# Feed-forward matmuls in pairs of 64-row halves, with one score pair at a time between them

## What is computed

```python
xn = _layernorm(x)
q, k, v = split(xn @ Wq + bq), split(xn @ Wk + bk), split(xn @ Wv + bv)
scores = jnp.einsum('bhnd,bhmd->bhnm', _rope(q), _rope(k)) / jnp.sqrt(256)
inter = jnp.einsum('bhnm,bhmd->bhnd', softmax(scores), v)
attn = merge(inter) @ Wo + bo
h = s0 * (concat([xn, -xn]) @ pm1(k0))      # pm1: True is 1, False is -1
h = s1 * (relu(h) * 2 @ pm1(k1))
h = s2 * (relu(h) * 2 @ pm1(k2))
out = x + attn + h                          # feed-forward 256 -> 1024 -> 1024 -> 256
```

## Time and profile before

| | us |
|---|---|
| median of 3 runs | 2984.65 (2983.89 to 2989.23) |
| the profiled execution | 2983.02 |
| its span, first to last instruction | 2981.2 |
| PE busy | 2785.1, 93% |
| ACT busy | 2146.0, 72% |
| DVE busy | 1057.8, 35% |
| mean granted TensorE clock | 0.973 of full |

### The profile page before, as it was taken

The page is one execution under the profiler, slowest core; times in us unless marked ns, Lnnn a source line. Parts: engine busy times, 40 slices in busy tenths (PEclk is TensorE's granted clock), DMA queues, the critical chain, the costliest instruction groups (busy, mean ns, idle before and its releaser), DMA issues.

```text
span 2981.2 us, 48065 instructions
## 1 busy us (share of the span) xinstructions
PE 2785.1 (93%) x16839; PEld 1300.0 (44%) x16839; DVE 1057.8 (35%) x1609; ACT 2146.0 (72%) x2301; POOL 376.9 (13%) x309
## 2 busy tenths in 40 slices
PE   6777299999999999999999999999999999999997
PEld 3443144444444444444444444444444444444444
DVE  7999422323232323232232323232322223232322
ACT  4446277777777777777777777777777777777773
POOL 5888300000000000000000000000000000000000
PEclk9999699999999999999999999999999999999998
DMA  6666411112121212112122212121211212221212
GB/s 200 196 196 191 131 43 44 43 47 55 47 50 41 61 45 73 49 46 62 48 65 54 69 44 69 39 75 45 63 53 51 62 47 66 54 69 43 74 35 96
DMA packets 279684, 211.62 MB, mean 71 GB/s; under 512 B 183616, under 2 KB 227392, under 8 KB 272960
## 3 DMA queue, kind: packets, MB, share of 16 engines
q1 hardware_dynamic: 271040, 200.30, 24.6%
q10 hardware_dynamic: 8448, 8.39, 0.9%
HBM read 132.08 MB, written 76.55 MB: 70 GB/s over the span
## 4 chain that ended last, share of the span: by engine, by line
PE 79%; issue 6%; DMA 2%; SPq 1%; DVE 1%; POOL 0%; ACT 0%; POOLq 0%; DVEq 0%
PE ps_o L871 29%; PE ps_f L903 27%; PE ps_s L856 22%; SPq L749 1%; DMA y<-rest_sum_d 1%; POOL heads L962 0%; PE ps_f L943 0%; DMA q_rows<-row_shift 0%; DVE sums L983 0%; DMA rest_sum_d<-rest_sum 0%; DMA probs<-rest_sum_d 0%; DMA heads_t<-heads 0%; DVE k_rows L1029 0%; PE ps_o L943 0%; DVE h_hi L993 0%
## 5 line engine op out<-in xcount | busy, mean ns | idle before, releaser
L831 ACT ACTIVATE probs<-ps_s 128x1024 f32<-128x1024 f32 x2048 | 1985.8, 1022 | 620.5 <-PE ps_s L856 620.5
L871 PE MATMUL ps_o<-probs,v_ones 128*32 128x512 f32 x8192 | 992.0, 602 | 0.0
L856 PE MATMUL ps_s<-q_rows,k_rows 50*128 50x512 f32 x4096 | 797.0, 462 | 61.9 <-DMA q_rows<-row_shift 32.6
L856 PEld LDWEIGHTS ps_s<-q_rows,k_rows 50*128 50x128 f32 x4096 | 337.2, 185 | 717.3 <-ACT probs L831 468.1
L993 DVE TENSOR_SCALAR h_hi<-ps_f 128x512 fp32r<-128x512 f32 x256 | 175.7, 686 | 1102.1 <-PE ps_f L903 1101.7
L903 PE MATMUL ps_f<-h_hi,ffn_w 128*128 128x512 f32 x1024 | 425.8, 416 | 0.0
L903 PE MATMUL ps_f<-h_lo,ffn_w 128*128 128x512 f32 x1024 | 415.6, 406 | 0.0
L871 PEld LDWEIGHTS ps_o<-probs,v_ones 128*32 128x32 f32 x8192 | 214.6, 109 | 453.0 <-issue 449.6
L962 POOL TENSOR_TENSOR heads<-heads,sums 128x512 f32<-128x512 f32 x64 | 85.9, 1342 | 2240.1 <-DVE sums L983 2240.1
L903 PEld LDWEIGHTS ps_f<-h_hi,ffn_w 128*128 128x128 f32 x1024 | 192.1, 188 | 101.7 <-issue 70.1
L983 DVE RECIPROCAL sums<-sums 128x128 f32<-128x128 f32 x256 | 225.0, 920 | 1.8
(11 more groups left out here) (87 smaller groups left out, 1382.5 us busy)
## 6 DMA issues: line engine op xcount, KB each, us to landing
k_rows<-k_parts SPq DMA_DIRECT2D x128, 256.0 KB
q_rows<-q_parts SPq DMA_DIRECT2D x384, 64.0 KB
q_parts<-parts SPq DMA_DIRECT2D x32, 512.0 KB, 3.7
k_parts<-parts SPq DMA_DIRECT2D x32, 512.0 KB, 4.5
k_rows<-k_parts SPq DMA_DIRECT2D x128, 128.0 KB
x_chunk<-in_x ACTq DMA_DIRECT2D x16, 512.0 KB, 4.1
xn_t<-xnT SPq DMA_DIRECT2D x16, 512.0 KB, 4.4
v_heads<-v_sb SPq DMA_DIRECT2D x16, 512.0 KB, 5.3
```

Source lines behind the costliest of these rows:

```text
L831: nc.scalar.activation(probs[:, s % PBUF, half * 2 * C:(half + 1) * 2 * C], ps_s[:, half].rearrange("p c n -> p (c n)"), ACT.Exp, scale=SC ...
L856: last = nc.tensor.matmul(ps_s[:, half, w], k_rows[rows, u, t * P:(t + 1) * P], q_rows[rows, u, half], start=True, stop=True)
L871: last = nc.tensor.matmul(ps_o[32 * c:32 * c + 2 * DH], v_ones[:, u, t], probs[:, s % PBUF, c * C:(c + 1) * C], start=(t == 0), stop=(t == ...
```

## The change

The feed-forward matmuls of 128 rows become **pairs** of matmuls of 64 rows. In a pair, the first matmul uses rows 0 to 63 and adds into one bank, and the second uses rows 64 to 127 and adds into another bank, which belongs to the next group. After half of its pairs the two groups swap the row halves (`phase`), so that each bank gets both halves of its sum. PE waits at the swap until the matmuls of the first phase are complete (`half_done`). A pair of groups takes as many pairs as it took matmuls before (8, 32 and 32 in the three layers). The projection keeps 128 rows.

A cycle now gives its four score pairs one by one, and between them stand three **visits** of feed-forward pairs. Their sizes are in `VISITS`: 2, 2, 4 in each of the four cycles of the first layer; two projection cycles with 0, 4, 0 matmuls, which stay empty in passes without projection; then 6 pairs in a cycle of the second layer and 8 in every fifth; and 12, 10 and 10 of the half-width pairs in a cycle of the third. DVE takes both groups of a pair after the second is done. In the new file `scores` is at line 859, `beside` at 887 and `one_pass` at 934.

```diff
-def turns(with_projection):
...
+FIRST, PROJECT, SECOND, THIRD = range(4)
...
+VISITS = {FIRST: [2, 2, 4], PROJECT: [0, 4, 0], SECOND: [2] * 13 + [3] * 2, THIRD: [4] * 4 + [3] * 4 + [4]}
...
-            def scores(i, s):
+            def scores(i, s, half):
...
-                for half in range(2):
-                    pe.wait_ge(probs_ready, 2 * STEPS * i + (2 * s + half + 1))
-                    for w in range(2):
...
+                pe.wait_ge(probs_ready, 2 * STEPS * i + (2 * s + half + 1))
+                for w in range(2):
...
+                banks = (first % BANKS, (first + 1) % BANKS)
                 if m == 0:
 
-                    pe.wait_ge(group_used, before + (k_th + 2 if k_th < BANKS - 1 else k_th + 1))
-                    if n == 0:
+                    pe.wait_ge(group_used, before + (first + 3 if first == 0 else first + 2))
...
+                if m == size:
+                    pe.wait_ge(half_done, 2 * swap)
+                for w in range(2):
+                    side = (w + phase) % 2
+                    rows = slice(GROUP_ROWS * w, GROUP_ROWS * (w + 1))
+                    n = 2 * pair + side
+                    if layer == FIRST:
+                        to, lhs, rhs = ps_f[:, banks[side]], w0[rows, k, n * P:(n + 1) * P], (xT_hi, xT_lo)[low][rows, k]
...
+                    last = nc.tensor.matmul(to, lhs, rhs, start=(m == 0), stop=(m == 2 * size - 1))
+                    if m == size - 1:
+                        last.then_inc(half_done, 1)
+                    if m == 2 * size - 1:
+                        last.then_inc(group_done, 1)
...
+                for c in range(STEPS // 2):
+                    s = FFN_FROM + 2 * c
+                    more = s < STEPS or not last
+                    if more:
+                        scores(i, s, 0)
+                    for layer, pair, m in TURNS[projects][3 * c]:
+                        beside(i, projects, layer, pair, m)
+                    if more:
+                        scores(i, s, 1)
+                    for layer, pair, m in TURNS[projects][3 * c + 1]:
+                        beside(i, projects, layer, pair, m)
+                    if more:
+                        scores(i, s + 1, 0)
+                    for layer, pair, m in TURNS[projects][3 * c + 2]:
+                        beside(i, projects, layer, pair, m)
+                    if more:
+                        scores(i, s + 1, 1)
                     weigh(i, s - 2)
                     weigh(i, s - 1)
...
-                dve.wait_ge(group_done, groups_before(i, projects) + (k_th + 1))
+                dve.wait_ge(group_done, groups_before(i, projects) + (k_th + 1 if n >= GROUPS else k_th + 2 - k_th % 2))
```

More of the change, by code:

```diff
@@ L61, with pairs, number, cycles @@
 GROUPS = SUMS + TT
-def turns(with_projection):
[L66 to L87, removed]
+SWAPS = FT + TT // 2
+FIRST, PROJECT, SECOND, THIRD = range(4)
+def pairs(layer):
+    return {FIRST: FT // 2, PROJECT: TT // 2, SECOND: FT // 2, THIRD: TT // 2}[layer]
+def number(layer, pair, side):
+    return {FIRST: 0, PROJECT: GROUPS, SECOND: FT, THIRD: SUMS}[layer] + 2 * pair + side
+VISITS = {FIRST: [2, 2, 4], PROJECT: [0, 4, 0], SECOND: [2] * 13 + [3] * 2, THIRD: [4] * 4 + [3] * 4 + [4]}
+def cycles(with_projection):
+    visits, ends, order = [], [], []
+    for layer in (FIRST, PROJECT, SECOND, THIRD):
+        for pair in range(pairs(layer)):
+            at = 0
+            for count in VISITS[layer]:
+                present = layer != PROJECT or with_projection
+                visits.append([(layer, pair, at + m) for m in range(count)] if present else [])
+                at += count
+            ends += [[] for _ in VISITS[layer][::3]]
+            if layer != PROJECT or with_projection:
+                ends[-1] = [number(layer, pair, side) for side in range(2)]
+                order += ends[-1]
+    assert len(ends) == STEPS // 2
+    return visits, ends, {n: k for k, n in enumerate(order)}
+TURNS, ENDS, ORDER = zip(*(cycles(p) for p in (False, True)))
 def groups_before(i, projects):
@@ L903, in beside @@
[L903 to L916 removed]
+                if pair == 0 and layer in (SECOND, THIRD) and m in (0, 2 * (FT - 2)):
+                    sums_of = (FIRST, SECOND)[layer == THIRD]
+                    needed = FT // 2 - 1 if m else FT // 2 - 2
+                    pe.wait_ge(group_used, before + (ORDER[projects][number(sums_of, needed, 1)] + 1 + BANKS))
@@ new lines, in beside @@
+                if layer == PROJECT:
+                    side, k = m // DT, m % DT
+                    t = 2 * pair + side
+                    last = nc.tensor.matmul(ps_f[:, banks[side], 0:D], headsT[:, k, t * P:(t + 1) * P], wo[:, k],
+                                            start=(k == 0), stop=(k == DT - 1))
+                    if k == DT - 1:
+                        last.then_inc(group_done, 1)
+                    return
+                size = 2 * (DT if layer == FIRST else FT)
@@ L917, in one_pass @@
                     weigh(i, s - 2)
                     weigh(i, s - 1)
+            w0, w1, w2 = w["w0"], w["w1"], w["w2"]
             pe.sem_inc(pv_done, PBUF)
-            scores(0, 0)
-            scores(0, 1)
+            for s in range(FFN_FROM):
+                scores(0, s, 0)
+                scores(0, s, 1)
             pe.wait_ge(consts_loaded, 48)
```

58 lines of the change are left out of this document (21 added, 37 removed).

## The result

| | before | after |
|---|---|---|
| median, 5 runs each on one chip | 2984.65 (2983.89 to 2989.23) | 3001.54 (2999.9 to 3006.57) |
| the profiled execution | 2983.02 | 3001.54 |
| its span | 2981.2 | 2999.7 |
| mean granted TensorE clock | 0.973 | 0.966 |

The ratio is 1.0054, 95% interval 1.0039 to 1.0069: slower by about 16 us, small but clear of the 0.2% (6 us) that the prediction took for what a measurement can tell. The forecast was 2986, no change, with a range of its own of 2976 to 2998 and one of 2972 to 3030 with two rivals in it.

What follows compares the result with a forecast made beforehand. A chain from PE to ACT and back was taken to bound cycles at 4.90. Passes with projection -5.5, without +3.8, no-loop returns +2, empty cycles +3: +3.3 on 2983.02 gives 2986; own range 2976 to 2998, with two rivals 2972 to 3030.

Steps and rivals of the forecast that it cites:

- B: Rival: the two halves' loads don't lie side by side in a stream; third-layer pairs take 0.21, 3017 us; chance 0.12.
- C: Rival: the longer loop body makes PE wait a second time for instructions at returns with projection, 3028 us; chance 0.05.
- the first layer: Four pairs before the fourth score pair make these cycles 5.14, 0.24 above the chain; 0.96 us a pass.
- the empty cycles: Two cycles without feed-forward work in passes without projection: the clock may fall; 0 to 12 us in all, taken as 3.
- PE's excess: In passes with projection, PE's own work costs 1.42 us a pass above the chain, which the change removes.
- Second-layer cycles of 4.90: The PE-ACT chain keeps these cycles at 4.90; the 0.4 us PE saves turns into waiting for ACT.
- pairs 0.23 apart: A feed-forward pair of 512 columns costs 0.23 us, as one full matmul does; bounds 0.21 and 0.46.
- The two cycles where no loop returns: Into pass 4 and the last pass, PE waits for the first groups to be emptied: 1 us each, 2 in all.
- A: Rival: PE's total is the true bound, so saved switches shorten all 512 cycles by 0.4, 2778 us; chance 0.11.
- D: Rival: a feed-forward pair costs clearly more than a full matmul: 0.34 gives 3150 us, 0.46 gives 3470; chance 0.10.
- Two float32 matmuls take 0.59 together ... so about 0.22 each.: Projection cycles: four matmuls at about 0.22 and two switches end near 1.73, so the cycle stays at 4.90.
- Cycles 6 to 30: Second- and third-layer cycles of a pass: 11.2 us less in all with projection, no change without.

Runs made afterwards that it cites:

- e1: The changed kernel without 6 of the 32 pairs of each second-layer pair of groups (384 in all): 2998.71, ratio 1.0042 to the kernel before.
- e5: The kernel before, without 3 of 16 matmuls in every second-layer group (384 in all): 2975.75, ratio 0.9968.
- e4: The changed kernel with a cycle's two weighings apart, each behind one step's scores: 2999.75, ratio 1.0045 to the kernel before.
- e10: The changed kernel with projection moved later, empty cycles filled, and uneven second-layer cycles (8 pairs, weighings together; 4 pairs, apart): 2863.61, ratio 0.9598 to the kernel before.
- e6: The changed kernel with the empty cycles of passes without projection given to the last two pairs of first-layer groups: 2991.81, ratio 1.0031 to the kernel before.
- e7: The changed kernel with the two weighings apart only from cycle 6 of a pass on: 3006.16, ratio 1.0086 to the kernel before.
- e8: e7 with e6's filling, and second-layer groups ending in other cycles than a head does: 2986.21, ratio 1.0014 to the kernel before.

## Why the forecast was right, and where it was off

**What the number owes to luck.** The forecast was no change within 0.2%, and the change is a slowdown of 0.5%. Inside the forecast the prediction gave 0.13 to slower. The median of 3001.54 lies 3.5 us above the forecast's own range (2976 to 2998); it is inside 2972 to 3030 only because that range was made to hold rivals B and C, and neither of them came. The low end of the own range was mis-added as well: with nothing for the first layer and the empty cycles, and all of PE's excess gone, the sum gives 2983 - 17 + 2 = 2968, below the low end of the wider range too.

**The frame held.** Second-layer cycles of 4.90 with ACT as the last releaser, first-layer ones of 5.14, pairs 0.23 apart: each was forecast and is in the rows. The two cycles where no loop returns are 0.93 longer (6.07 for 5.14), forecast 1.0. Cycles with 8 pairs take 4.93 for 4.90. e1 and e5 show by taking work away that the chain bounds, e4 and e10 by breaking it, and the last pass of either kernel by a chain 0.08 shorter.

**The rivals.** A (2778) is out by the result itself, in which the switches are gone and the cycles stay at 4.90, and by e1. B is out by the third layer's timeline, where the pairs stand 0.12 apart:

```profile
1647.94 0.28 PE L928 MATMUL ps_f<-ffn_w,h_hi 64*128 64x256 f32 x2
...
1648.06 0.28 PE L928 MATMUL ps_f<-ffn_w,h_lo 64*128 64x256 f32 x2
...
1648.18 0.28 PE L928 MATMUL ps_f<-ffn_w,h_hi 64*128 64x256 f32 x2
```

C didn't come: the loop's return with projection has one gap, as before. The rows name "issue" for such a gap; that PE waits for instructions in it isn't shown. D's price of 0.34 for a pair appears only behind a wait (from the score pair at 1551.19 to the next at 1551.53); in a stream it is 0.23. The Trainium skill's page "TensorE: Matmul & The Clock Gate" (Part 3, The mechanism), which the prediction weighed, says that weight loads overlap running matmuls only where the row group differs. That doesn't fit these rows: in the pair after the pair the row groups are the same, and the loads stay hidden.

**The steps that failed** are sizes, and together they are the 15.8 us between the forecast's +3.3 and the 19.1 of the table:

- *"Two float32 matmuls take 0.59 together ... so about 0.22 each."* The two records of the earlier trace rows were one matmul. A float32 matmul of 256 columns leaves two records, and eight records (four matmuls) start 0.22 apart, so a matmul costs 0.43 and the switches the rest of the 1.92. (`turns` in the kernel before counts it as two full ones, which was there to be seen.) A projection cycle takes 5.11, not 4.90. That is 0.21 x 24 = 5.0 us. The other 1.4 of the 6.4 missed in this row of the table is mostly the wait for the load of `y`, which both kernels have in some passes: about 12 us before (what cycle 4 takes beyond its usual 5.19), 13 after (what it takes beyond 5.11). The Trainium skill ("FP8 and Floating Point Precision", TensorE Precision Notes) says that true float32 takes four passes through the array. Four times 256 columns at 2.4 GHz would be 0.43, an estimate from that page, and the trace agrees with 0.43.
- *"I take 3, nearer to nothing, because the weighing in such a cycle is as dense as before."* The empty cycles cost 6.2 in this execution: 0, 3.1, 1.5 and 1.6 in the four passes. The dense weighing didn't keep the clock up in three of them. It lay inside the bounds of 0 and 12. e6 shows that the clock is the cause; what tips it, with nearly the same waits in the first pass, stays open.
- *Cycles 6 to 30* gained 0.6 us less than forecast with projection, and without it lost 1.0: 0.03 in each cycle with 8 pairs, 64 of them, is 1.9, more than both.
- *The start of `attend`* had no term. It cost 2.5 in this execution: there the clock is at half when the first pairs come (0.43 from pair to pair), and it rose some 5 us later than before. That is mostly chance. In the profiles of e1, e6, e7 and e8, whose queue is the same there, the place lies from 0.5 under to 2.0 over before, and in that of e5, which has the queue of the kernel before, it is 2.0 over.

*The first layer* came out at +12.2 with projection for +11.1. The forecast's +3.8 without it came out at +5.1, of which 2.3 is in the first cycle after a loop's return; that cycle differs from pass to pass in both kernels (8.0 to 9.3 before, 9.1 to 10.1 after), and why was not tried.

## What to carry to other kernels

Before valuing a saving on the busiest engine, take one period of the steady state and ask what released the instruction that ends last. Here PE was busy for 93% before, after, and in a version 4% faster. Where two bounds lie within 2% of each other (a chain through another engine, and the engine's own work), relief of one alone buys next to nothing (0.3% in e5); work can then be placed unevenly, so that long blocks lie under the chain and short ones where the chain is cut. And each gain brings forward the next late thing: make a ledger by place of cycle, since e7 and e8 won what they were built for and lost it again in other cycles, for the most part on one late load.

## What the runs showed that I had not expected

- A float32 matmul stands in the trace as two records with the shape of the whole (eight for the projection's four, sixteen for the eight of two weighings). Count records against the program before dividing a duration by them.
- After waits of 0.96 and 0.41 in a cycle with no feed-forward work the clock was at 1.2 GHz for the next 7 us in one pass. It stayed at 2.4 in both such cycles of the first pass (waits of 0.89 and 0.41) and in the first one of the fourth (0.96 and 0.41). With one or two pairs in each visit (e6), and waits of 0.27 and 0.19 at the same points, it stayed at 2.4 in all eight cycles, and so it did in e4, with no pairs but the weighings apart.
- The wait for the load of `y`, 6.0 us from issue to landing in the pass shown, cost up to 6.4 us of a cycle (11.5 for 5.11): a lower clock behind it (0.63 in the last 6.67 us) came on top of PE's idle time of about 4.
- Whether weighings stand together or apart costs PE at least 0.26 a cycle (5.19 against 4.93 with 8 pairs), and still pays by 0.16 to 0.65 where PE has room.
- ACT starts an exponential 0.08 sooner after its scores where its instructions stand outside its loop, and the cycles that the chain bounds are 0.08 shorter there. What the 0.08 would be worth in all the cycles was not tried.
